# Filler products left out, a spread of values moved to another queue, and two additions swapped

## What is computed

```python
# layer 0
cmod = silu(c) @ w_ada + b_ada                       # six vectors of each batch entry
x_mod = ln(x) * (1 + scale_msa) + shift_msa
k, q, v = split(x_mod @ w_qkv, 3)
y = softmax(q / 8 @ k.T) @ v                         # by head
x = x + gate_msa * (y @ w_proj + b_proj)
x = x + gate_mlp * (gelu(modulate(ln(x)) @ w_mlp1 + b_mlp1) @ w_mlp2 + b_mlp2)
# layer 1, two directions d, keys and values of the first 20 tokens
self_feat = concat(x, q_exp) @ W_self.T + b_self
output = self_feat
for d in range(2):
    w = softmax(masked(q_d @ k_d.T) + label_bias_d)
    output = output + (w @ kv) @ Wout_d + bout_d     # by head
x = x + relu(output)
```

## Time and profile before

| | us |
|---|---|
| median of 3 timed runs | 97.1 (97.0 to 97.69) |
| the profiled execution | 95.63 |
| its span, first to last instruction | 93.8 |

### The profile page before, as it was taken

How to read it: one execution, slowest core, us unless ns; L and a number is a source line. 1 busy time by engine, 2 the same in 40 slices (tenths; PEclk the granted TensorE clock), 3 DMA queues, 4 the chain that set the end, 5 groups by cost and what they waited for, 6 DMA issues and landing times.

```text
span 93.8 us, 4196 instructions
## 1 busy us (share of the span) xinstructions
PE 83.7 (89%) x1802; PEld 67.5 (72%) x1802; DVE 71.7 (76%) x183; ACT 55.7 (59%) x127; POOL 46.1 (49%) x72
## 2 busy tenths in 40 slices
PE   4959989999999989989999999999998999968900
PEld 4849967676676778768888877988876688647800
DVE  0766289989699997689169388997989879568791
ACT  4880386939999729572972305789244597208620
POOL 6697015457922005546242461081553977971680
PEclk9999999999999999999999999999999999999995
DMA  1989999400000000000000001100200212120203
GB/s 35 246 203 367 372 232 241 112 3 7 0 7 7 0 7 3 0 0 0 7 0 0 5 20 31 30 10 22 55 9 0 57 31 64 27 54 14 61 0 112
DMA packets 3778, 5.75 MB, mean 61 GB/s; under 512 B 720, under 2 KB 2896, under 8 KB 3632
## 3 DMA queue, kind: packets, MB, share of 16 engines
q1 hardware_dynamic: 3496, 5.31, 20.6%
q10 hardware_dynamic: 264, 0.18, 0.7%
HBM read 4.22 MB, written 0.52 MB: 51 GB/s over the span
## 4 chain that ended last, share of the span: by engine, by line
PE 65%; DVE 15%; issue 6%; POOL 5%; ACTq 4%; ACT 2%; POOLq 0%; DVEq 0%
PE ps_s L1043 8%; PE ps_b L964 8%; PE ps_b L944 7%; PE ps_b L919 6%; PE ps_b L895 5%; PE ps_b L1069 5%; ACTq L752 4%; PE ps_b L1061 4%; PE ps_b L970 4%; PE ps_b L1091 3%; PE ps_b L912 3%; POOL E L676 3%; DVE neg_max L1445 3%; PE ps_b L1100 2%; PE ps_b L952 2%
## 5 line engine op out<-in xcount | busy, mean ns | idle before, releaser
L1227 ACT ACTIVATE PT<-ps_b 120x384 f32<-120x384 f32 x16 | 7.4, 487 | 8.6 <-PE ps_b L1061 4.6
L1141 ACT ACTIVATE hidden<-ps_b,cols 128x256 f32<-128x256 f32 x16 | 7.0, 474 | 6.5 <-PE ps_b L964 6.5
L856 POOL TENSOR_TENSOR rstd<-var_eps,minus_half 128x2 f32<-128x2 f32 (+1 forms) x9 | 6.0, 668 | 6.3 <-DVE var_eps L1261 6.2
L784 POOL TENSOR_TENSOR Kb<-k_raw,head_mask 128x640 f32<-128x640 f32 x4 | 5.0, 1258 | 8.1 <-ACT k_raw L1156 5.4
L1436 DVE TENSOR_TENSOR E<-ps_s,bias_rep 128x640 f32<-128x640 f32 x8 | 6.6, 823 | 3.0 <-PE ps_b L1061 1.7
L964 PE MATMUL ps_b<-xm,w_rest_sb 128*128 128x256 f32 x32 | 8.6, 385 | 0.0
L676 POOL TENSOR_TENSOR E<-E,neg_max 128x640 f32<-128x640 f32 x5 | 6.4, 1271 | 4.4 <-DVE neg_max L1445 3.9
L1043 PE MATMUL ps_s<-Kb,home_b 32*32 32x80 f32 x512 | 7.4, 239 | 0.7 <-DVE E L1436 0.7
L970 PE MATMUL ps_b<-hidden,w_rest_sb 128*128 128x256 f32 x32 | 7.6, 386 | 0.0
L647 POOL TENSOR_TENSOR xm<-xm,cmod 128x256 f32<-128x256 f32 (+1 forms) x6 | 3.5, 586 | 8.3 <-DVE xm L1283 8.3
L1043 PEld LDWEIGHTS ps_s<-Kb,home_b 32*32 32x32 f32 x512 | 5.7, 103 | 2.4 <-issue 1.5
(11 more groups left out here) (120 smaller groups left out, 218.0 us busy)
## 6 DMA issues: line engine op xcount, KB each, us to landing
w_rest_sb<-in_w_rest SPq DMA_DIRECT2D x1, 1088.0 KB, 7.9
home_a<-in_adj SPq DMA_DIRECT2D x2, 448.0 KB, 12.3
Vz<-v_raw SPq DMA_DIRECT2D x16, 33.8 KB
xT<-in_xT SPq DMA_DIRECT2D x1, 512.0 KB, 9.8
home_a<-in_adj SPq DMA_DIRECT2D x1, 512.0 KB, 12.7
out<-x_tok SPq DMA_DIRECT2D x3, 128.0 KB, 1.9
x_tok<-in_x_tok SPq DMA_DIRECT2D x1, 256.0 KB, 5.2
w_ada_sb<-in_w_ada SPq DMA_DIRECT2D x1, 256.0 KB, 5.6
```

The lines of the kernel that those rows point to most:

```text
L856: ins = pool.tensor_tensor(rstd[:, layer, g0:g1], var_eps[:, layer, g0:g1], minus_half[:, 0:g1 - g0], ALU.pow)
L1141: return act.activation(hidden[:, slot_of(h), j, 0:n], ps[:, 0:n], ACT.Gelu_apprx_tanh, bias=cols[:, R_MLP1 + j:R_MLP1 + j + 1])
L1227: ins = act.activation(PT[0:KR, key % 3, 0:CH, :], ps[0:KR, 0:CH * P].rearrange("p (j t) -> p j t", t=P), ACT.Exp)
```

## The change

It empties `FILL` (both entries), gives `('spread', ('v1', 3, 1))` to SP's queue, and swaps the two additions: `ya` now adds the self part, `yb` the second direction. `ORDER` is as it was. The place in which fillers would be issued changes too, but there are none left. `WARM = 5` stays.

```diff
-FILL = {('k', 0): 12, ('xnT', 2): 2}
+FILL = {}
...
- ('spread', ('v1', 3, 1)): 'act',
+ ('spread', ('v1', 3, 1)): 'sp',
...
+        def add_self(engine, name, g):
+            n = UNITS.index((1, 0, g))
+            for s in fresh(name, ("mult", pair_of(n)), ("take", (("sbtok", mid_of(g)), 0))):
+                engine.wait_ge(*s)
+            return engine.tensor_tensor(y01[:, g, 0, :], y01[:, g, 0, :], sb_tok[:, g, :], ALU.add)
+
         def add_dirs(engine, name, g):
-            n = UNITS.index((1, 1, g))
-            for s in fresh(name, ("mult", pair_of(n)), ("mult", pair_of(UNITS.index((1, 0, g))))):
+            for s in fresh(name, ("ya", g), ("mult", pair_of(UNITS.index((1, 1, g))))):
                 engine.wait_ge(*s)
             return engine.tensor_tensor(y01[:, g, 0, :], y01[:, g, 0, :], y01[:, g, 1, :], ALU.add)
...
                 elif stage == "ya":
-                    ins = add_dirs(pool, "pool", key)
+                    ins = add_self(pool, "pool", key)
                 else:
                     assert stage == "yb"
-                    ins = add_self(pool, "pool", key)
+                    ins = add_dirs(pool, "pool", key)
...
-                for i in range(FILL.get(name, 0)):
-                    pe.matmul(ps[:, 0:P], ones[:, :], ones[:, :], start=True, stop=True)
+                if not ahead_of_scores(name):
+                    for i in range(FILL.get(name, 0)):
+                        pe.matmul(ps[:, 0:P], ones[:, :], ones[:, :], start=True, stop=True)
```

More of the change, by code:

```diff
@@ L896, in turn_many, with ahead_of_scores @@
                 return ins
+            def ahead_of_scores(name):
+                return ORDER.index(("dense", name)) < min(ORDER.index(o) for o in ORDER if o[0] == "scores")
             def dense_product(name):
@@ L1010, in _ @@
                 if stage == "dense":
+                    if ahead_of_scores(key):
+                        for i in range(FILL.get(key, 0)):
+                            pe.matmul(ps_s[:, i % HJ, 0:P], ones[:, :], ones[:, :], start=True, stop=True)
                     ins = dense_product(key)
@@ L1426, in _ @@
                 elif stage == "ya":
-                    ins = add_dirs(dve, "dve", key)
+                    ins = add_self(dve, "dve", key)
                 elif stage == "badd":
@@ L1492, in _ @@
                 elif stage == "yb":
-                    ins = add_self(dve, "dve", key)
+                    ins = add_dirs(dve, "dve", key)
                 else:
```

## The result

| | before | changed |
|---|---|---|
| median of 20 timed runs each, us | 97.05 | 97.39 |
| the profiled execution, us | 95.63 | 98.61 |
| its span, us | 93.8 | 96.9 |

The ratio is 1.012, interval 1.0085 to 1.0155. By it the change made the kernel 1.2% slower, where 0.4 us of gain was forecast; by the medians of all twenty it is 0.34 us or 0.35% slower.

A forecast was written before the change was run, and what follows sets the result against it. The prediction took most of the kernel to be a queue of PE work. It summed -0.6 us at the start, +0.2 at the end and nothing for the swap to -0.4, from 97.1 to 96.7 us, range 95.4 to 98.1.

The forecast's parts named there:

- Where the start goes from 10.5 to 7.9 and half is given back: Start: without fillers `k 0` starts 2.67 us earlier; at the low clock the second `cmod` ends only 1.24 earlier.
- From there to `xnT 3`: Start, after `cmod`: DVE bounds, then PE at the low rate; `xnT 3` starts at about 12.9, 1.15 us earlier.
- The rise of the clock: Start: the clock rises at 15.4, 3.4 us into PE's full stretch from 12.0, leaving 0.65 us gained, taken as 0.6.
- the fourth: Rival at the start: the clock's rise eats the gain exactly, the end adds 0.2, 97.3 us; chance 0.52 together with the forecast.
- the first: Rival at the start: the clock rises late, at 19.5, costing 1.4 us, 98.7 in all; chance 0.2.
- The gain of 1.1 on the way to `values 20`, and its loss there: End: ACT without issues lets PE gain 1.1 us; `values 20` then waits for SP's eight issues, net 0.2 later.
- The landing: End: the spread's last bytes come 0.75 to 1.0 us after SP's last issue, at 86.85 to 87.1.
- The swap at nothing: The two additions of y: both cost 0.33 us on DVE whichever operand comes, so swapping them changes nothing.
- The sum: Whole kernel: -0.6 us at the start and +0.2 at the end, -0.4 together, for a median of 96.7.

The follow-up runs named there:

- e1: The kernel before with `FILL` emptied and nothing else; ratio 1.0049 to before.
- e6: The kernel before with fillers only where PE waits: two products ahead of `xnT 0`, three of `k 0`, two of `xnT 2`; ratio 0.9858 to before.
- e9: The kernel before with the edits of e8 and e6 together; ratio 0.9756 to before.
- e11: The kernel before with only the last spread's part 1 moved to SP's queue, a repeat of e2; ratio 1.009 to before.
- e2: The kernel before with only the last spread's part 1 moved to SP's queue, five executions; ratio 1.0107 to before.
- e10: The changed kernel with six products of ones ahead of `values 20`; ratio 1.0104 to before.
- e8: The kernel before with the last spread's issues divided, six on SP and two on ACT; ratio 0.9908 to before.
- e3: The kernel before with only the two additions of y swapped; ratio 1.0024 to before.

## Why the prediction was wrong

**Where the start goes from 10.5 to 7.9 and half is given back:** right. `k 0` at 7.97 (7.87 predicted), the last of `cmod` from 9.38 to about 10.95 (10.95 predicted), and DVE's take of it 1.04 earlier than before (11.18 for 12.22). The 1.24 of the prediction compares the issue of the last product with an end that includes its drain (11.21 + 0.98), so it was 0.2 too much.

**From there to `xnT 3`:** mis-sized by 0.48. The term had it at 12.9, it started at 13.38 (before 14.05). `xnT 2` started at 12.13 and not at 12.0, and from there to `xnT 3` PE took 1.25 us. The sum gave that stretch 0.93 at the low level, which is what it took before, from 13.12 to 14.05, at the high level. It had counted the issuing of PE's instructions and left out what stands between them. The gain at that point was 0.67 and not 1.15.

**The rise of the clock:** mis-sized, and the step that turned the sign at the start. It was put at 15.4, as long behind the start of the gapless stretch as in before's one trace. Four traces without early fillers have it at 16.13 to 16.87, the changed kernel's at 16.42. At half a us for each, 1.0 us later is worth 0.5. With the 0.48 above, `scores 1` goes from 0.66 earlier to 0.33 later, which is where the changed kernel has it (16.99 for 16.66); e1 measured +0.49% for the whole start (0.08 to 0.91%). The rival that came nearest is the fourth, in which a rise at 16.7 eats the gain; the first wanted it behind 18 and put a loss of 1.4 on it, about three times of what e1 measured. The prediction cited the Trainium skill ("TensorE: Matmul & The Clock Gate", Part 1) for activity lifting the clock. The traces agree: the rise came at 9.28 to 10.50 in the six with twelve fillers ahead of `k 0` and at 16.13 to 16.87 in the four without. But e6 and e9 show that one trace can't say where it falls: the same start had it at 14.46 and at 17.26.

**The gain of 1.1 on the way to `values 20`, and its loss there:** right as a mechanism. The stall of `values 16` is gone, SP issues eight in 5.99 us (5.96 predicted), and PE waits for the landing. The landing is the term that was too small: 0.75 to 1.0 us behind the last issue's end was read from the last bytes, but PE waits for the semaphore, which comes later: in before's own trace its last event is at 85.29, 1.14 behind the end of ACT's issues. The eight end at 86.54 in e11, the last event of the semaphore is at 87.69, and PE goes on at 87.82, 1.28 behind the issues. That gives +0.5 instead of +0.2, which is what e11 has at `values 20`. In the changed kernel's trace two issues were long besides (1.20 and 1.28 us), which makes 7.07 of 5.96; it had been kept as a bound only.

**What the prediction had not at all:** that the clock can fall in or just behind the wait it predicted itself, of 1.1 us or more, when the last work still has to be done. It had reckoned with the clock at the start alone. Where the fall comes it costs 0.54 (e11) to 1.16 us (changed). As said, its share in the mean isn't shown.

**The swap at nothing:** 1.0024 with an interval around 1; nothing contradicts it.

**The sum:** -0.6 + 0.2 against about +0.5 and +0.9 measured apart. Both terms were differences of two sums that nearly cancel, and in both the part on the losing side was counted too small: at the start what stands between PE's instructions and the moment of the rise, at the end the landing and the fall of the clock. With the measured landing alone the end would have been +0.5 and the sum still -0.1; the sign needed the rise as well. How the 0.9% of e11 divides between the wait and the clock stays open.

## What to carry to other kernels

Fillers that warm TensorE belong where it waits anyway: with fourteen products, twelve of them ahead of the work that they delay, the kernel took 96.84 us in the median, and with seven in the waits 95.93 (e6). Their effect on the clock has to be judged over many executions, since the rise moved by 2.8 us between two traces of the same start. Before a transfer is moved to spare an engine its issues, count what each queue then issues one behind the other up to the last consumer; dividing four issues two and two took 0.9% off, all on one queue put 0.9% on. And a new idle stretch of TensorE is to be priced with the clock behind it, not only with its own length: it fell at 88.10 to 88.89 in the changed kernel, e2 and e11.

## What was not expected of the hardware

- The record of the granted clock has no entry before its first change. PEclk reads full from the beginning in every trace here, while the instructions of 128 columns run at 0.213 us each until the first entry. The spacing of equal products is the view to trust.
- A DMA issue of 0.71 us sometimes takes 1.2 to 1.9. In the changed kernel's trace the queue of instruction loads was active beside the last one, from a window of 0.6 us around its start:

```profile
q8 instruction: 1, 0.02, 12.7%
q1 hardware_dynamic: 27, 0.01, 8.0%
```

  The other long ones (1.20 at 82.10 here, 1.78 in e10, 1.68 and 1.23 in e8) also have such a load within 0.35 us before their start. That it is the cause was not tested. Such a load doesn't always lengthen an issue: in the changed kernel one came at 73.78, 0.28 us before the issue at 74.06, which took 0.71.
- In e3's trace the clock fell at 85.60, 0.11 us after the stall of 1.14 us in which PE stands still for ACT's issues as in before, and rose again at 89.01, with PE at work all the while:

```profile
84.30:85.49 1.19, 0.05 (x2) 0.01 (x1) 0.82 (x1) 0.55 (x2) 0.80 (x1) 1.00 0.23 50
85.60:89.01 3.41, 3.41 (x105) 3.00 (x106) 2.09 (x4) 1.98 (x6) 0.86 (x2) 0.50 0.18 48
```

  It took 97.62 us, with 0.982 of the clock granted over the span. Of 69 timed executions of the kernel before on four chips, 22 were granted just this share; they took 97.06 to 98.55 us, and the other 47 took 95.36 to 97.69. It is likely, though no trace of these is kept, that the clock fell behind the stall in them too. If so, the fall is a part of the kernel before in a third of its executions, the changed kernel's median of 97.39 lies within their range, and the loss of 1.2% is one against the executions of before in which the clock did not fall.
